# Last layer of a four-layer kernel: inverse norms of queries and keys by Newton rounds on VectorE in place of ScalarE's square root

## The reference, cut to what matters

```
def _l2norm(t):
    n = jnp.sqrt(jnp.sum(t * t, axis=-1, keepdims=True))
    return t / jnp.maximum(n, EPS)          # EPS = 1e-12
q = _l2norm(proj(Wq, bq))                   # 16 heads of 8 features
k = _l2norm(proj(Wk, bk))
v = proj(Wv, bv)
sim = jnp.einsum('bhid,bhjd->bhij', q, k)
attn = sim / scaling
out = jnp.einsum('bhij,bhjd->bhid', attn, v)
return out @ Wo + bo
```

## Time and profile before

| what | value |
|---|---|
| median of 3 runs | 662.57 us (659.83 to 668.09) |
| profiled execution: span from first to last instruction | 632.2 us |
| median of the runs less this span | 30.4 us |
| busy in the span | PE 537.4, DVE 452.7, ACT 393.8, POOL 377.5 us |
| mean granted clock of PE | 0.958 |

### The profile page before, as it was taken

One profiled execution on the slowest core, in us unless ns is written; L12 is line 12 of the kernel. 1 busy time (PEld: TensorE's weight loads), 2 busy tenths in 40 slices (PEclk: granted clock), 3 DMA queues, 4 the chain that ended last, 5 costly groups with the idle time before them and its releaser, 6 DMA issues. The chain is left out here.

```text
span 632.2 us, 10057 instructions
## 1 busy us (share of the span) xinstructions
PE 537.4 (85%) x3490; PEld 423.8 (67%) x3490; DVE 452.7 (72%) x801; ACT 393.8 (62%) x779; POOL 377.5 (60%) x296
## 2 busy tenths in 40 slices
PE   5999867587787878798787989698999988989997
PEld 2444556466675767576654867698788986775766
DVE  6799799999999998898385597153333575658662
ACT  3679899769979987455469496413221135748670
POOL 0588798989999996488540650772900771125430
PEclk9999788799899899999999799899999999999999
DMA  5036053345666640200070000610611210000002
GB/s 131 4 84 108 16 122 101 83 113 130 134 139 131 135 121 2 76 0 2 17 210 3 1 8 28 147 64 17 183 32 45 66 34 2 2 0 1 2 0 67
DMA packets 45819, 40.44 MB, mean 64 GB/s; under 512 B 12183, under 2 KB 32585, under 8 KB 45770
## 3 DMA queue, kind: packets, MB, share of 16 engines
q1 hardware_dynamic: 44746, 37.71, 25.2%
q0 software_dynamic: 1024, 2.10, 1.1%
HBM read 33.70 MB, written 6.09 MB: 63 GB/s over the span
## 5 line engine op out<-in xcount | busy, mean ns | idle before, releaser
L435 PE MATMUL bank<-all_ident,l0s_ring 128*128 128x128 f32 x512 | 72.9, 291 | 18.7 <-POOL l0s_ring L731 18.5
L435 PEld LDWEIGHTS bank<-all_ident,l0s_ring 128*128 128x128 f32 x512 | 61.8, 150 | 27.4 <-POOL l0s_ring L731 24.8
L860 DVE TENSOR_TENSOR_SCAN l0s_ring<-l_XM,l0s_ring,bank 128x512 f32<-128x512 f32 x62 | 74.6, 1254 | 1.8 <-PE bank L415 1.8
L731 POOL TENSOR_TENSOR l0s_ring<-l0s_ring,l0s_c_rest 128x1024 f32<-128x1024 f32 x32 | 66.3, 2092 | 7.9 <-DVE l0s_ring L860 3.6
L731 POOL TENSOR_TENSOR l0s_ring<-l0s_ring,all_XF 128x1024 f32<-128x1024 f32 x31 | 66.2, 2154 | 5.8 <-DVE l0s_ring L860 2.7
L415 PE MATMUL bank<-all_ident,all_XNT 128*128 128x128 f32 x312 | 50.0, 302 | 22.9 <-DVE l0s_ring L860 15.7
L607 ACT ACTIVATE all_XNT<-l_wraw,l_wins 128x256 f32<-128x256 f32 x156 | 66.1, 497 | 0.5 <-PE bank L415 0.4
L860 DVE TENSOR_TENSOR_SCAN l0s_ring<-bank,l0s_ring 128x512 f32<-128x512 f32 x50 | 60.2, 1244 | 5.1 <-ACT bank L586 2.5
L415 PEld LDWEIGHTS bank<-all_ident,all_XNT 128*128 128x128 f32 x312 | 39.3, 156 | 29.7 <-ACT all_XNT L607 12.7
L586 ACT ACTIVATE l_XM<-l_DT,l_negA 128x512 f32<-128x512 f32 x78 | 50.8, 712 | 0.6 <-DVE l0s_ring L860 0.6
L721 POOL TENSOR_TENSOR l0s_ring<-l_DTU,l0s_b_all 128x1024 f32<-128x1024 f32 x20 | 40.1, 2005 | 0.0
(11 more groups left out here) (442 smaller groups left out, 1497.7 us busy)
## 6 DMA issues: line engine op xcount, KB each, us to landing
l0s_c_rest<-bc_rows SPq DMA_DIRECT2D x16, 512.0 KB, 5.4
all_XF<-bc_rows SPq DMA_DIRECT2D x16, 512.0 KB, 5.3
l0s_b_all<-bc_rows SPq DMA_DIRECT2D x20, 256.0 KB, 6.0
l_wall<-in_L_ffn_W SPq DMA_DIRECT2D x14, 256.0 KB, 4.7
all_X<-in_L_attn_x SPq DMA_DIRECT2D x4, 256.0 KB, 3.5
gx<-l1m_TD SPq DMA_DIRECT2D x1, 1024.0 KB, 5.6
gy<-l1m_TD SPq DMA_DIRECT2D x1, 1024.0 KB, 8.6
out<-all_X SPq DMA_DIRECT2D x4, 256.0 KB, 2.3
```

The lines of the kernel that those rows point to most:

```text
L435: last = nc.tensor.matmul(y_of(k, j), hc[n % CRING][:, j, bass.ts(k, P)], S.ident[:, :], start=False, stop=(n % DS == DS - 1 and k % 2 == ...
L731: nc.gpsimd.tensor_tensor(hc[n % CRING][:, :, :], h(n)[:, :, :], wide(c_wide[p % HRING][:, n % 2, :]), ALU.mult).then_inc(hc_ready, 1)
L860: nc.vector.tensor_tensor_scan(h(n)[:, j, :], factor, added, before, ALU.mult, ALU.add).then_inc(h_ready, 1)
```

## The change

`heads_root` and the one-column Silu leave ScalarE's queue. VectorE no longer waits for ScalarE in `heads_inverse`, but works on its own sums: it raises `ss` to at least 1e-24, takes a first value of its inverse root by arithmetic on the bits of the number (the exponent is halved and negated), and improves it by three Newton rounds of three instructions each. Each of the eleven instructions waits for the one ahead of it, since it reads its result.

```
-                        def heads_root(b):
-                            act.wait_ge(summed, b + 1)
-                            nc.scalar.activation(nrm, ss, ACT.Sqrt).then_inc(rooted, 1)
...
-                            heads_root(b)
-                            nc.scalar.activation(spare[:, :], S.one_col[:, 0:1], ACT.Silu)
...
                         def heads_inverse(b):
-                            dve.wait_ge(rooted, b + 1)
+                            dve.wait_ge(summed, b + 1)
+                            nc.vector.tensor_scalar(ss, ss, L2_EPS * L2_EPS, None, ALU.max).then_inc(clipped, 1)
+                            dve.wait_ge(clipped, b + 1)
                             if b:
                                 dve.wait_ge(unit, b)
-                            nc.vector.tensor_scalar(nrm, nrm, L2_EPS, None, ALU.max).then_inc(clipped, 1)
-                            dve.wait_ge(clipped, b + 1)
-                            nc.vector.reciprocal(rn3, nrm).then_inc(rn_ready, 1)
+                            nc.vector.tensor_scalar(rn3.bitcast(I32), ss.bitcast(I32), -0.5, ROOT_SEED, ALU.mult, ALU.add).then_inc(newton, 1)
+                            at = 3 * ROOT_ROUNDS * b
+                            for i in range(ROOT_ROUNDS):
+                                dve.wait_ge(newton, at + 3 * i + 1)
+                                nc.vector.tensor_tensor(nrm, rn3, rn3, ALU.mult).then_inc(newton, 1)
+                                dve.wait_ge(newton, at + 3 * i + 2)
+                                nc.vector.scalar_tensor_tensor(nrm, nrm, -0.5, ss, ALU.mult, ALU.mult).then_inc(newton, 1)
+                                dve.wait_ge(newton, at + 3 * i + 3)
+                                nc.vector.scalar_tensor_tensor(rn3, nrm, 1.5, rn3, ALU.add, ALU.mult).then_inc(rn_ready if i == ROOT_ROUNDS - 1 else newton, 1)
```

More of the change, by code:

```diff
@@ L1154 @@
 L2_EPS = 1e-12
+ROOT_SEED, ROOT_ROUNDS = 1597463007.0, 3
 EARLY = 4
@@ L1921, in layer1_phases @@
                 less, shift = (ph.sb(n, [P, TILES]) for n in ("less", "shift"))
-                spare = ph.sb("spare", [P, 1])
                 mx, tot, rtot = (ph.sb(n, [QW, 2, GW]) for n in ("mx", "tot", "rtot"))
@@ L1968, in layer1_phases @@
                     ph.sem(n) for n in ("gate_done", "up_done", "silu_done", "hid_done", "down_done", "stored"))
-                (late_loaded, heads_made, qkv_done, biased, squared, summed, rooted, clipped, rn_ready, unit, bo_added, q_turned, qhT_ready, kv_done,
+                (late_loaded, heads_made, qkv_done, biased, squared, summed, newton, clipped, rn_ready, unit, bo_added, q_turned, qhT_ready, kv_done,
                  kvT_ready, m2_done, m2_ready, o3_done, finished, written) = (
-                    ph.sem(n) for n in ("late_loaded", "heads_made", "qkv_done", "biased", "squared", "summed", "rooted", "clipped", "rn_ready", "unit",
+                    ph.sem(n) for n in ("late_loaded", "heads_made", "qkv_done", "biased", "squared", "summed", "newton", "clipped", "rn_ready", "unit",
                                         "bo_added", "q_turned", "qhT_ready", "kv_done", "kvT_ready", "m2_done", "m2_ready", "o3_done", "finished", "written"))
```

## The result

| | before | changed |
|---|---|---|
| median of 4 runs | 665.29 us | 673.32 us |
| lowest to highest | 659.83 to 668.09 us | 669.87 to 675.95 us |
| ratio | | 1.013, 95% interval 1.0088 to 1.0173 |

The change makes the kernel slower: by 8 us between the medians, and by 1.3% in the ratio of the runs. That is clear of the spread of the runs and under 2%.

What follows compares the result with a forecast made beforehand. The prediction took VectorE's longer chain before `hidden`, with PE waiting behind it, as the bound: 6.4 us of chain plus 2.6 us of clock gave +9.0, so 662.6 + 9.0 = 671.6 us, range 664 to 677.

Steps and rivals of the forecast that it cites:

- chain, clip to last step: VectorE's eleven dependent instructions in each round take 3.37 us, against 1.18 from clip to reciprocal before.
- round 1, `hidden` later: In round 1 `hidden` starts 1.91 us later: 2.19 us of extra chain less 0.28 us of idle time.
- round 2: `hidden` starts later by the whole extra chain, 2.19 us, as no idle time stood there.
- round 3: `hidden` starts 1.01 us later: 2.19 us of extra chain less 1.18 us of idle time.
- round 4 and on: The inverse ends 1.30 us later: 2.19 us of extra chain less the 0.89 us wait for the root.
- sum at full clock: VectorE's delays over the four rounds add up to 6.4 us, bounds 4.2 and 8.3.
- clock: PE's granted clock falls after idle stretches of some 3 us in two rounds, 1.3 us each: 2.6 us, bounds 0 and 6.8.
- The dear case: Rival: the clock falls in all four rounds and VectorE's steps are dear: +15.1 us, 677.7 us; chance 0.13.
- its nearest rival: The clock holds despite PE's longer idle stretches, leaving only +6.4 us: 669.0 us; chance 0.27.
- ScalarE's share: ScalarE's lateness is worth at most 2.35 us of VectorE's time: 0.28 + 0 + 1.18 + 0.89 over four rounds.
- The rival in which ScalarE ends the waits: Kernel gets faster, as ScalarE ends the waits at `hidden` of rounds 1 and 3 and round 4's clip: 660.2 us; chance 0.05.
- The span: Profiled length of the whole kernel before, 632.2 us; the median of the runs was put 30.4 us above it.

Runs made afterwards that it cites:

- fifth and tenth experiment: Changed kernel with root and one-column Silu put back into ScalarE's queue and the clip waiting for the root, profiled twice: tails 59.63 and 58.07 us.
- ScalarE's part alone: Kernel before without ScalarE's root, Silu and their table loads, VectorE keeping one clip and one reciprocal, of the sums themselves: tail 47.80 us, ratio 0.9971.

## Why the prediction was right

| term | predicted | measured |
|---|---|---|
| chain, clip to last step | 3.37 us | 3.44 |
| round 1, `hidden` later | 1.91 | 5.28 - 3.39 = 1.89 |
| round 2 | 2.19 | 5.28 - 3.22 = 2.06 |
| round 3 | 1.01 | 3.94 - 2.99 = 0.95 |
| round 4 and on | 1.30 | 24.11 - 22.77 = 1.34 |
| sum at full clock | 6.4 | 6.28 |
| clock | 2.6 | 3.83 and 4.03 |
| whole | +9.0 | +10.1 in the tail, +8.0 between the medians |

The round terms are read in the kernel with PE kept busy, where the clock doesn't blur them, from `out` to `hidden` and, in the last row, from the `hidden` of round 3 to the end. They are its own steps and hold one by one. The whole, +9.0 us, lies between the +10.1 of the tail and the +8.0 of the medians, but the medians can't judge the terms: the interval of the ratio reaches from about 6 to 11.5 us. The eleven instructions, their durations and gaps came out as the nearest rows said: 0.29 us a step and 0.33 from one start to the next. The integer form, for which no row stood, took 0.23 to 0.25 us; the clip's 0.22 was the right neighbour. The dear case, six instructions at 0.35 us, is out. The Trainium skill, VectorE: DVE Perf Modes, in its section on the TRN2 errata, also has a formula for adding two float tensors, elements plus 151 cycles at 0.96 GHz, which it calls exact for 512 and 2,048 elements. As an estimate from it an instruction on 128 elements takes 0.29 us; the trace's 0.29 us agrees with that one, and not with the 58 cycles of its table.

**The clock** was the step that decided between the forecast and its nearest rival (669.0). The mechanism was as forecast: the clock fell in just the two rounds with stretches of 3 us and in neither of the others. Its size was low. I took 1.3 us for each, since the projections are paced by VectorE's biases as well; it was 1.42 in round 1 and 2.41 in round 2, where the clock was down for 7 us and not for 3.5, part of it before PE could work. In round 1 the eight matmuls of the projections took 4.43 in place of 3.02 us, which is all of it. The bound of 1.7 us for one round was too low. The reason for expecting a fall was also weaker than it looked. It took stretches of 3 us to be safe because one of 1.84 us was followed by a fall; stretches of 2.70 and 2.72 us were not, in the fifth and tenth experiment. That all four stretches of 2.98 us were followed by one is what was measured, and no rule that was known beforehand.

**ScalarE's share** was 2.35 us in the prediction, in the form of idle times that the longer chain fills. Together with the chain that holds: two of the three terms are filled, and the third, the 0.89 us wait of round 4, measured 0.86. As a gain of its own it would have been too high, 1.76 us. The rival in which ScalarE ends the waits and the time drops to 660.2 had 0.6 us too much, and the experiment with ScalarE's part alone shows that even the 2.35 us were not to be had: idle time before an instruction is close to an upper bound, since the next to be late stands behind it. It isn't a strict one. In round 1 `hidden` came 0.37 us earlier for 0.28 us of idle time, because it starts 0.08 us before the reciprocal has ended (613.79 against 613.87).

**The span** was misread. I set the median 30.4 us above the span and took that as what lies around it. A run's time stands about 2 us above its span (675.32 and 673.6, 661.86 and 659.6). The first profile of before came from an execution with a short upstream part. Nothing in the sum used it but the addition of a constant to both sides, so the difference stands.

What was expected to show it did: nine Newton instructions at 0.29, `copy_x` behind PE's turn (ScalarE's wait ends on PE at 609.89), no idle time ahead of `hidden`, PE idle for 2.98, 2.98, 1.65 and 1.3 us (3, 3, 2 and 1.3 predicted), and a clock near 0.5 behind the long ones. From `out` of round 1 to that of round 2 are 1.88 us more than before at full clock (14.08 against 12.20; about 2 predicted), and 3.30 more with the slow clock.

## What to carry to other kernels

Moving work from an engine that looks late to one that looks idle pays only if it lands where the second engine waits. Read the idle time right at the place of insertion: here it was 0.28, 0, 1.18 and 0.89 us against 2.26 us of added chain, while 1.54 us (in round 2) lay unused just ahead of `out`. Price small dependent instructions by their number and kind (on 128 elements 0.33 us for each product here, 0.23 to 0.28 for the clip and the integer form, against 0.95 for the reciprocal), and add what TensorE's clock loses once the new wait becomes long. Compare a short stage between two fixed steps of its own, not spans.

## What the runs showed of the hardware

- One program's clock record is not fixed: at the same place the clock held behind an idle stretch of 1.85 us in PE in one execution and fell behind 1.86 us in another. Nor does the length of the stretch alone decide: it fell behind 1.84 us, held behind 2.00 (twice), 2.70 and 2.72, and fell behind 2.76 (once) and 2.98 (four of four).
- Sixty useless transposes in PE's waits delayed nothing and gave back 3.83 us.
- Between groups of runs the whole kernel before differed by 28 to 30 us (medians 637.65 and 665.37, a single run of 667.76), while its tail, profiled twice, repeated to 0.01 us. The traces place the difference in two stretches ahead of the last stage; the cause stays open.
